# Last pass of a graph network kernel: in each step VectorE and ScalarE take the parts that TensorE reads ahead of squares, results and the root

## The reference, cut to what matters

```python
def layer(h, W, b):
    h = h @ W.T
    msg = h[src] * norm[:, None]
    agg = jax.ops.segment_sum(msg, dst, num_segments=n)   # a node's own row included
    return jax.nn.relu(agg + b)
...
h = layer(h, W3, b3)
...
x = _layernorm(x + h, axis=-1)
```

## Time and profile before

| | us |
|---|---|
| median of 3 runs | 3882.38 |
| lowest, highest | 3879.71, 3885.96 |
| span of the profiled execution | 4682.8 |

### The profile page before, as it was taken

One profiled execution on the slowest core, in us unless ns is written; L12 is line 12 of the kernel. 1 busy time (PEld: TensorE's weight loads), 2 busy tenths in 40 slices (PEclk: granted clock), 3 DMA queues, 4 the chain that ended last, 5 costly groups with the idle time before them and its releaser, 6 DMA issues. The chain is left out here.

```text
span 4682.8 us, 91816 instructions
## 1 busy us (share of the span) xinstructions
PE 3627.1 (77%) x25918; PEld 3425.2 (73%) x25918; DVE 2940.1 (63%) x8173; ACT 2975.1 (64%) x6203; POOL 2514.8 (54%) x2663
## 2 busy tenths in 40 slices
PE   3988888889954443887787776888887868888887
PEld 3888888888844443777777776777777758887877
DVE  5898888888867774444444434444444447767766
ACT  2767766666758874555555554555555648888878
POOL 4666655556536664555555535555555455555552
PEclk8999999999965556888888887888888879999998
DMA  4555545545449996555555544555555457777775
GB/s 108 148 157 153 146 146 151 148 141 154 138 162 345 346 343 207 171 162 161 160 163 161 160 150 143 167 164 161 167 161 161 150 171 241 236 232 241 245 234 179
DMA packets 654365, 858.88 MB, mean 183 GB/s; under 512 B 136335, under 2 KB 515882, under 8 KB 654256
## 3 DMA queue, kind: packets, MB, share of 16 engines
q1 hardware_dynamic: 556954, 652.14, 42.9%
q0 software_dynamic: 94080, 205.08, 15.6%
q10 hardware_dynamic: 3222, 0.43, 0.1%
HBM read 639.00 MB, written 257.52 MB: 191 GB/s over the span
## 5 line engine op out<-in xcount | busy, mean ns | idle before, releaser
L1454 DVE TENSOR_TENSOR gcn_agg_lo<-gcn_agg_ps,gcn_agg_hi 128x1024 fp32r<-128x1024 f32 x196 | 240.0, 1225 | 1037.8 <-ACT gcn_agg_hi L1486 828.2
L493 POOL DMA_INDIRECT rows<-ga_scratch,node_i x490 | 492.8, 1006 | 479.7 <-DVE gcn_rows_lo L1463 297.4
L493 POOL DMA_INDIRECT rows<-x_scratch,node_i x490 | 490.6, 1001 | 478.9 <-DVE gcn_rows_lo L1463 304.7
L1486 ACT CAST gcn_agg_hi<-gcn_agg_ps 128x1024 fp32r<-128x1024 f32 x196 | 197.8, 1009 | 841.3 <-remote 804.5
L493 POOL DMA_INDIRECT rows<-gb_scratch,node_i x490 | 490.8, 1002 | 404.9 <-DVE fin_rows_lo L1643 232.6
L493 POOL DMA_INDIRECT rows<-x_in,node_i x490 | 541.3, 1105 | 163.7 <-issue 127.2
L525 PE MATMUL gcn_agg_ps<-gcn_select,gcn_rows_hi 128*128 128x256 f32 (+2 forms) x1960 | 594.5, 328 | 31.6 <-DVE gcn_rows_lo L1463 17.7
L539 PE MATMUL gcn_h_ps<-g_hi,gcn_agg_hi 128*128 128x256 f32 x1568 | 475.3, 303 | 157.3 <-ACT gcn_h_ps L1478 91.1
L525 PE MATMUL gcn_agg_ps<-gcn_select,gcn_rows_lo 128*128 128x256 f32 (+2 forms) x1960 | 567.7, 322 | 7.2 <-issue 7.0
L539 PE MATMUL gcn_h_ps<-g_lo,gcn_agg_hi 128*128 128x256 f32 x1568 | 466.9, 298 | 55.8 <-issue 53.1
L539 PE MATMUL gcn_h_ps<-g_hi,gcn_agg_lo 128*128 128x256 f32 x1568 | 463.3, 295 | 51.0 <-issue 49.5
(11 more groups left out here) (197 smaller groups left out, 12525.9 us busy)
## 6 DMA issues: line engine op xcount, KB each, us to landing
own<-x_t_in SPq DMA_DIRECT2D x196, 256.0 KB
h_scratch<-h2t SPq DMA_DIRECT2D x196, 256.0 KB
h2t_in<-h_scratch SPq DMA_DIRECT2D x98, 512.0 KB, 5.1
x_sb<-x_q_in SPq DMA_DIRECT2D x98, 512.0 KB, 6.9
x_scratch<-x SPq DMA_DIRECT2D x98, 512.0 KB, 5.6
gcn_own<-x_scratch SPq DMA_DIRECT2D x98, 512.0 KB
ga_scratch<-gcn_h SPq DMA_DIRECT2D x98, 512.0 KB
gcn_own<-ga_scratch SPq DMA_DIRECT2D x98, 512.0 KB
```

The source lines that it names most:

```text
L493: pool.indirect_dma_start(out=c["rows"][0:n, slot, b], out_offset=None, in_=source[:, :], in_offset=bass.IndirectOffsetOnAxis(ap=c["node"] ...
L1454: nc.vector.tensor_tensor(agg_lo[:, b], agg_ps[:, b], agg_hi[:, b].bitcast(F32), ALU.subtract)\
L1486: nc.scalar.copy(agg_hi[:, b], agg_ps[:, b]).then_inc(agg_rounded, 1)
```

## The change

Only the order within a step of `last_pass` is changed, on two engines; no instruction, wait, buffer or transfer is added or taken away. New order:

- VectorE: `rs` (7), `shift` (7), `res` (5), `agg_lo` (3), `less_mean` (5), `select` (1), `rows_lo` (1), `power` (6).
- ScalarE: relu (5), `agg_hi` (3), `rows_hi` (1), `spread` (6), `y` (7), `sd` (6).

```diff
@@ VectorE, step
                         nc.vector.reciprocal(rs[:, b], sd[:, b]).then_inc(shift_ready, 1)
-                    if quad := at(1):
-                        if quad.has(2):
-                            dve.wait_ge(agg_done, quad.before(2))
-                        select_columns(nc, c, quad, select[:, quad.b])
                     if quad := at(7):
...
                         nc.vector.tensor_scalar(less_mean[:, b], total[:, b], -1.0 / D, None, ALU.mult)\
                             .then_inc(mean_ready, 1)
-                    if quad := at(6):
-                        b = quad.b
-                        dve.wait_ge(squared, quad.done())
-                        if quad.has(2):
-                            dve.wait_ge(sd_ready, quad.before(2))
-                        nc.vector.scalar_tensor_tensor(out=power[:, b], ...)
+                    if quad := at(1):
+                        if quad.has(2):
+                            dve.wait_ge(agg_done, quad.before(2))
+                        select_columns(nc, c, quad, select[:, quad.b])
                     if quad := at(1):
                         b, s = quad.b, quad.slot
                         dve.wait_ge(rows_rounded, quad.done())
...
                         last.then_inc(rows_ready, 1)
+                    if quad := at(6):
+                        b = quad.b
+                        dve.wait_ge(squared, quad.done())
+                        if quad.has(2):
+                            dve.wait_ge(sd_ready, quad.before(2))
+                        nc.vector.scalar_tensor_tensor(out=power[:, b], ...)
@@ ScalarE, step
                         nc.scalar.copy(agg_hi[:, b], agg_ps[:, b]).then_inc(agg_rounded, 1)
+                    if quad := at(1):
+                        b, s = quad.b, quad.slot
+                        act.wait_ge(gathered[s], quad.landed(BLOCKS))
+                        if quad.has(2):
+                            act.wait_ge(agg_done, quad.before(2))
+                        nc.scalar.copy(rows_hi[:, b], c["rows"][:, s]).then_inc(rows_rounded, 1)
                     if quad := at(6):
...
                         last.then_inc(squared, 1)
-                    if quad := at(1):
-                        ... rows_hi as above
-                    if quad := at(6):
-                        b = quad.b
-                        act.wait_ge(power_ready, quad.done())
-                        if quad.has(2):
-                            act.wait_ge(shift_ready, quad.before(2) * 2)
-                        nc.scalar.activation(sd[:, b], power[:, b], ACT.Sqrt, scale=1.0 / D).then_inc(sd_ready, 1)
                     if quad := at(7):
...
                         last.then_inc(y_ready, 1)
+                    if quad := at(6):
+                        b = quad.b
+                        act.wait_ge(power_ready, quad.done())
+                        if quad.has(2):
+                            act.wait_ge(shift_ready, quad.before(2) * 2)
+                        nc.scalar.activation(sd[:, b], power[:, b], ACT.Sqrt, scale=1.0 / D).then_inc(sd_ready, 1)
```

More of the change, by code:

```diff
@@ L1630, in step @@
                             .then_inc(mean_ready, 1)
+                    if quad := at(1):
[4 more added lines that the diff above has]
+                        b, s = quad.b, quad.slot
+                        dve.wait_ge(rows_rounded, quad.done())
+                        for k in range(BLOCKS):
+                            last = nc.vector.tensor_tensor(rows_lo[:, b, k], c["rows"][:, s, k],
+                                                           rows_hi[:, b, k].bitcast(F32), ALU.subtract)
+                        last.then_inc(rows_ready, 1)
                     if quad := at(6):
@@ L1671, in step @@
                         last.then_inc(squared, 1)
-                    if quad := at(1):
-                        b, s = quad.b, quad.slot
-                        act.wait_ge(gathered[s], quad.landed(BLOCKS))
-                        if quad.has(2):
-                            act.wait_ge(agg_done, quad.before(2))
-                        nc.scalar.copy(rows_hi[:, b], c["rows"][:, s]).then_inc(rows_rounded, 1)
-                    if quad := at(6):
-                        b = quad.b
-                        act.wait_ge(power_ready, quad.done())
-                        if quad.has(2):
-                            act.wait_ge(shift_ready, quad.before(2) * 2)
-                        nc.scalar.activation(sd[:, b], power[:, b], ACT.Sqrt, scale=1.0 / D).then_inc(sd_ready, 1)
                     if quad := at(7):
```

## The result

The changed kernel takes 3932.09 us (median of 4 runs, 3931.48 to 3938.74), the kernel before 3881.05 beside it: a ratio of 1.0136, 95% interval 1.0124 to 1.0148, or +51 us. Forecast was +37, range 3872 to 3958. The span of its profiled execution is 3929.7 us, 1.8 us under that execution's own time of 3931.48. The 800 us by which the profiled execution of before stood over its timed runs have no counterpart here.

What follows compares the result with a forecast made beforehand. ScalarE, at 7.05 us a quad, was taken to bound the timed last pass; a 7.48 us loop adds 0.43 over 93 steps, +40, or +37 after TensorE's gaps: 3882.4 + 37 = 3919 us, range 3872 to 3958.

Steps and rivals of the forecast that it cites:

- The 800 us: Profiled span of 4682.8 us over the timed median of 3882.38: 800.4 us taken as absent when no profile is taken.
- two regimes: Last pass: with gaps, TensorE sets 9 us a quad; without them, ScalarE 7.05, said to hold nearly always when timed.
- discount of 1 in 14: Timed runs keep 63 of 863 us of gaps, so the loop's +40 us becomes +37.
- 863 us: Estimated gap excess in the profile: 338 us in each of two convolution passes plus 187 in the last pass.
- The loop: Last pass: sd (root), relu, res, agg_lo, less_mean, select, rows_lo, power, sd; 7.48 us against ScalarE's 7.05, +40 us.
- The edits taken to cost nothing: Last pass: earlier agg_lo, rows_hi and y, and rows_lo before power, cost nothing; agg_lo gains at most 5.3 us.
- The rule on the shared port: Select meeting a gather held up to 1.00 us: loop 8.27, +113 us; said not to be borne out by the trace.
- A: Rival: TensorE's gaps still rule the timed last pass and hide the loop; no change, 3882; 0.15 together with D.
- B: Rival: after late sums the new order recovers about 0.41 us each; faster, 3866; chance 0.11.
- C: Rival: loop hops at upper bounds, or select held more by gathers; 7.91 us or over, 3962; chance 0.12.
- D: Rival: waits cost less, loop 7.1 to 7.2 us; under 10 us, no change seen; 0.15 together with A.
- the profiled pass would stay near 871 us: Sign: the profiled last pass, ruled by TensorE's gaps, keeps its length within 15 us; loss shows only in timed runs.

Runs made afterwards that it cites:

- second profile of before: Unedited kernel before, profiled a second time: 3889.33 us for that execution, span 3887.6, beside a median of 3884.69.
- version with a shorter relu: Kernel before in its old order, ScalarE's relu taking three of four tiles and VectorE the fourth: 3863.46 us, ratio 0.9952.
- power out: Changed kernel with power moved ahead of select and rows_lo on VectorE (also called power early): 3898.82 us, ratio 1.0036.
- the two kinds in turns: Changed kernel with power ahead of select and rows_lo, and those two taken in turns, block by block: 3884.47 us, ratio 1.0002.
- the hold gone: Changed kernel with VectorE's and ScalarE's last-pass steps written out, and select and rows_lo in turns, block by block: 3893.09 us, ratio 1.0025.

## Why the prediction was right, and where it was short

**What bounds the kernel: right, and stronger than stated.** ScalarE at 7.05 us a quad, TensorE at 6.83. The second profile of before has ScalarE busy 655.5 of 660 us, and the version with a shorter relu gains what the estimate from that bound gives (-19 both times).

**The reading of the two regimes: right in its use, wrong in a reason.** The prediction set the 800 us against the gaps of three passes and concluded that the timed runs are in ScalarE's regime. They are. But the excess wasn't what a profile costs: the spans of the twelve other profiled executions are all within 2 us of their own times. It was one disturbed execution. The discount of 1 in 14 came from a 6.22 us quad of the convolution passes, read at their end; in the second profile those quads take 6.22 to 7.86 in the middle of the pass, 6.64 on average, so part of the 863 us was never excess, and the steps of the last pass are 7.05 all through. The discount was therefore a term of -3 us that should have been nought.

**The loop: right.** It exists (root waits for power in each step), both of its closing points are needed (new order on VectorE alone: +224; on ScalarE alone: 0), and select or power taken out of its chain undoes it (with power out 14 us stay, which are the held gathers').

**Its length: this is the term that was mis-sized.** Measured over 65 steps of the changed kernel, mean of the starts' differences, against what was added; the last column is the changed kernel with its steps written out:

| hop | predicted | measured | written out |
|---|---|---|---|
| root to relu | 0.10 | 0.19 | 0.11 |
| relu to res | 1.14 | 1.31 | 1.04 |
| res to agg_lo | 1.61 | 1.61 | 1.61 |
| agg_lo to less_mean, to select | 1.20 | 1.22 | 1.21 |
| select | 1.48 | 1.40 | 1.47 |
| rows_lo | 1.68 | 1.68 | 1.68 |
| power to root | 0.27 | 0.24 | 0.18 |
| loop | 7.48 | 7.65 | 7.30 |

Every hop that is an instruction's own length was right to 0.1. Relu to res and root to relu were not, together 0.26 short. Select and power to root had been taken 0.11 too long, so the sum came out only 0.17 short; that much of its closeness is luck. For relu to res I had two rows, 1.14 and 1.48, and took the lower, arguing the higher away; four values occur, by the place in the program loop's turn. For root to relu I used a pair of rows (sd to y) that never has the program loop's edge between it. 93 x 0.60 = +56 us from the measured length, against +51 measured; from the 7.48, +40 without the discount.

**The edits taken to cost nothing:** rs and shift lie under the relu, as said (3509.26 and 3509.48, res at 3510.83). agg_lo earlier gave nothing. TensorE's spare time was taken for harmless, and it is: it is early at every dense part and waits for agg_lo, 41.8 us over 3200 to 3860, without the end moving.

**The rule on the shared port.** The Trainium skill, on the page "SBUF — State Buffer" (section on the two sides of SBUF), has the loser of the port pair that VectorE and GpSimd share blocked fully, for a whole instruction of the other, in the cases that it names; no run here shows whether select is one of them. The prediction set that against the trace for select, with a loop of 8.27. The measured select is 1.40, and the loop 7.65, so the measurement decides against a full block of select. A hold did show, in the other direction, and wasn't in the prediction at all: a gather held by a rows_lo that stands directly behind select. In the changed kernel itself it hardly matters: 22 of the pass's 490 gathers, none of them after 3440 us, because GpSimd then waits for rows_lo to free a slot and so starts its five gathers just behind it.

**The rivals.** A (gaps rule in the timed runs) fell with the second profile. B (recovery) needed late sums; there were none: select waits for the sum in no step of the loop. C (dear loop) named two upper hops; one of them, relu to res at 1.48, was half true (1.31). D fell.

**The signs foretold.** Root waiting 0.3 to 0.5: 0.29 to 0.54 in the rows shown. VectorE idle before res about 1 us: 0.65 to 1.19. Steps of 7.4 to 7.6: 7.46 to 8.00, 7.65 on average, so mostly above. Select's waits for the sum, 57 us before, were to shrink: none is left. That the profiled pass would stay near 871 us didn't come true, since it hung on the disturbed execution.

## What to carry to other kernels

Where two engines work through a step in a fixed order, follow each chain of waits around until it comes back to where it began, one step later: if the last instruction of one engine's step is waited for by the last of the other's, and early work of the next step in turn waits for the other engine, the step is as long as the whole chain, even when neither engine is full. Work that stood under a wait (select, here) is free only there; moved ahead of the instruction that the other engine wants, it is paid in full. Add to such a chain what each hop behind a wait costs in a program loop, measured and at every place of its turn, and check a profiled execution's span against its own time before a regime is read from it.

## What the runs showed of the hardware that was not expected

- Where five `tensor_tensor` on two SBUF operands stand directly behind five `tensor_scalar` (select, then rows_lo), many gathers that GpSimd starts while the `tensor_tensor` run are held until these have ended: with power early 71 of 104, in the changed kernel 22 of 43. 1.00 us became 1.5 to 2.6, and the end came 2.63 us after a row of 1.68 began. With a short instruction ahead of the row instead (power or less_mean) none of 503 was longer than 1.30, and with the two kinds in turns none was longer than 1.35. What decides isn't known.
- In a program loop, res behind its wait for relu started 0.1 to 0.4 us later than in written-out code (1.15 to 1.42 against 1.04), and the turn of the program loop cost 0.3 us when the engine had nothing queued (root to relu 0.42 against 0.11). Where the engine had work queued, writing out 84 steps gave nothing (ratio 1.0001).
- Two engines can lock at a common period that is neither's own: 7.30 us in each step with VectorE and GpSimd slowing each other (select 1.47, one gather 1.80), 7.11 with the hold gone.
- One profiled execution of the kernel before was 800 us longer than its runs, with gaps on TensorE and a granted clock of 0.91 in the last pass, where a second had none and 1.00. Its cause wasn't found.
